# Mixture of experts, Mamba block, mixture of experts on one core: scan states in SBUF, masking on ScalarE, decays two steps ahead, residual adds on TensorE

## The reference

```python
# xn = rmsnorm(layernorm(x)) on 256 features; D_INNER 512, D_STATE 16, D_CONV 4, DT_RANK 64
x_in, z = split(xn @ in_proj_w.T)
x_conv  = silu(causal_conv4(x_in) + conv_b)
dt_low, B_ssm, C_ssm = split(x_conv @ x_proj_w.T)         # 64, 16, 16
dt = softplus(dt_low @ dt_proj_w.T + dt_proj_b);  A = -exp(A_log)
h  = h * exp(dt_t * A) + (dt_t * u_t) * B_t               # for every t; 512 x 16 states
y  = sum_s h[:, s] * C_t[s]  + x_conv * D
x  = x + (y * silu(z)) @ out_proj_w.T                     # x here is the layernormed input
h  = rmsnorm(x);  x = x + relu(h @ c_fc_w.T)**2 @ c_proj_w.T
```

## Time and profile before

| | us |
|---|---|
| median of 3 runs | 2183.04 |
| lowest and highest | 2175.22, 2190.57 |
| the profiled execution, its time | 2182.28 |
| its span, first to last instruction | 2180.4 |
| first scan to last product's end | 591.8 to 1607 |
| VectorE busy over the span | 1709.5 (78%) |
| TensorE busy | 1725.6 (79%) |
| GpSimd busy | 1242.9 (57%) |
| ScalarE busy | 977.6 (45%) |

### The profile page before, as it was taken

One profiled execution on the slowest core, in us unless ns is written; L12 is line 12 of the kernel. 1 busy time (PEld: TensorE's weight loads), 2 busy tenths in 40 slices (PEclk: granted clock), 3 DMA queues, 4 the chain that ended last, 5 costly groups with the idle time before them and its releaser, 6 DMA issues. The chain is left out here.

```text
span 2180.4 us, 35658 instructions
## 1 busy us (share of the span) xinstructions
PE 1725.6 (79%) x10728; PEld 1411.5 (65%) x10729; DVE 1709.5 (78%) x2990; ACT 977.6 (45%) x1507; POOL 1242.9 (57%) x751
## 2 busy tenths in 40 slices
PE   5279999993886878879787787877577379999996
PEld 5279999993344546545464554545456269999996
DVE  4857666665498999989999999989955757766665
ACT  2333333331465566566666656665431323333331
POOL 1257455555476767767676676767631246545555
PEclk8589999997877898989999898988686579999998
DMA  6244343343343434434344443443412334333342
GB/s 193 79 120 105 69 86 82 82 70 90 121 137 126 140 127 141 136 122 143 127 136 127 137 136 127 136 128 136 142 36 97 97 102 106 81 74 87 82 78 26
DMA packets 161018, 237.96 MB, mean 109 GB/s; under 512 B 29370, under 2 KB 85296, under 8 KB 160304
## 3 DMA queue, kind: packets, MB, share of 16 engines
q1 hardware_dynamic: 130096, 198.84, 28.7%
q0 software_dynamic: 30720, 36.53, 10.1%
HBM read 202.57 MB, written 38.34 MB: 110 GB/s over the span
## 5 line engine op out<-in xcount | busy, mean ns | idle before, releaser
L1291 POOL TENSOR_TENSOR m_dB<-m_DTU,m_BC 128x1024 f32<-128x1024 f32 x256 | 604.0, 2362 | 308.0 <-DVE PS L1397 307.5
L1397 DVE TENSOR_TENSOR_SCAN PS<-PS,m_ST,m_dB 128x512 f32<-128x512 f32 x512 | 628.3, 1271 | 58.7 <-POOL m_dB L1291 27.1
L1110 ACT ACTIVATE PS<-m_DT,m_A 128x512 f32<-128x512 f32 x512 | 351.1, 690 | 361.3 <-DVE PS L1397 360.1
L1101 PEld LDWEIGHTS PS<-keep_ident,m_G 128*128 128x128 f32 x2048 | 254.9, 153 | 207.8 <-DVE m_G L1406 168.2
L1101 PE MATMUL PS<-keep_ident,m_G 128*128 128x128 f32 x2048 | 313.5, 297 | 90.2 <-DVE m_G L1406 89.7
L1406 DVE TENSOR_TENSOR m_G<-PS,m_BC 128x512 f32<-128x512 f32 x512 | 340.8, 673 | 10.3 <-PE PS L1101 10.2
L603 PE MATMUL PS<-e_xh,e_wh 128*128 128x256 f32 x1008 | 295.0, 293 | 0.5 <-DVEq L491 0.2
L603 PE MATMUL PS<-e_xl,e_wh 128*128 128x256 f32 x1008 | 289.0, 287 | 0.0
L603 PE MATMUL PS<-e_xh,e_wl 128*128 128x256 f32 x1008 | 288.8, 287 | 0.0
L660 ACT ACTIVATE e_hh<-e_u 128x512 fp32r<-128x512 f32 x252 | 157.9, 633 | 281.1 <-DVE e_u L716 280.9
L621 PE MATMUL PS<-e_wh,e_hh 128*128 128x256 f32 x1008 | 281.4, 279 | 0.0
(11 more groups left out here) (200 smaller groups left out, 2908.1 us busy)
## 6 DMA issues: line engine op xcount, KB each, us to landing
m_BC<-bc_rows SPq DMA_DIRECT2D x512, 256.0 KB, 3.3
layer_raw<-w SPq DMA_DIRECT2D x64, 512.0 KB, 3.9
xrows<-r_xn SPq DMA_DIRECT2D x16, 512.0 KB, 4.2
keep_X<-x SPq DMA_DIRECT2D x4, 1024.0 KB, 9.6
sums<-keep_X SPq DMA_DIRECT2D x4, 1024.0 KB, 11.1
out<-keep_X SPq DMA_DIRECT2D x4, 1024.0 KB, 11.0
keep_X<-sums SPq DMA_DIRECT2D x3, 1024.0 KB, 13.4
e_xin<-xrows,e_gix POOLq DMA_INDIRECT x160, 3.3
```

Of the source, the lines that this page charges most:

```text
L1101: last = M(PS[:, B_Y + j, ts], G[:, s % 2, j, ts], C["ident"][:, :], is_transpose=True, start=False, stop=(s == DS - 1 and a == CTT - 1))
L1110: return nc.scalar.activation(out, in_, func, **kw)
L1291: G_.tensor_tensor(dB[:, s % 2, :, :], DTU[:, es, :], BC[:, s % NBC, 0:1, :].to_broadcast([P, 2, CT]), ALU.mult).then_inc(dB_ok, 1)
L1397: V.tensor_tensor_scan(PS[:, B_H + j, :], PS[:, B_DA + j, :], dB[:, s % 2, j, :], ST[:, s, e:e + 1], ALU.mult, ALU.add).then_inc(scanned, 1)
```

## The change

- The scans write a new SBUF tensor `HS` (two buffers of two blocks), and the products read it there; PSUM banks 4 and 5 become free and hold a second pair of decays, which ScalarE computes two steps ahead.
- The masked copy of the last state becomes a ScalarE activation with a 0/1 scale (`keep`), behind that step's decays; a scan waits for the `keep` of two steps back.
- `G` has four buffers for two.
- `out` and `pj`: TensorE first multiplies the residual rows by the identity into the bank and then adds the projection onto it; ScalarE copies the bank out. VectorE has no instruction in the tables any more.
- `v`: the 1/256 goes into ScalarE's squares, eps is added by GpSimd.
- To make room, `T3` and `HID` share one tensor (`TH`), and `hT` is `xrT`.

```diff
-        mask = sb("mask", [P, MCH + 1], U32)
-        fmask = sb("fmask", [P, MCH])
+        fmask = sb("fmask", [P, MCH + 1])
...
-        G = sb("G", [P, 2, 2, CT])
+        NG, NH = 4, 2
+        G = sb("G", [P, NG, 2, CT])
+        HS = sb("HS", [P, NH, 2, CT])
...
-        B_DA, B_H, B_Y = 2, 4, 6
+        B_DA, B_Y, AHEAD = 2, 6, 2
...
         BACK = {
...
-            ("out", 0): (4, _, 5, _), ("out", 1): (6, _, 7, _), ("sq", 0): (_, 9, _, _), ("v", 0): (_, _, 10, 12),
+            ("out", 0): (4, 5, _, _), ("out", 1): (6, 7, _, _), ("sq", 0): (_, 9, _, _), ("v", 0): (_, _, _, 11),
...
-            ("fc", 3): (27, 28, _, _), ("q", 1): (_, 28, _, _), ("pj", 0): (29, _, 30, _), ("pj", 1): (30, _, 31, _),
+            ("fc", 3): (27, 28, _, _), ("q", 1): (_, 28, _, _), ("pj", 0): (29, 30, _, _), ("pj", 1): (30, 31, _, _),
...
                     if kind == "out":
                         wait_read(pe, k, ("g", 2), ("g", 3), into=p)
+                        pe.wait_ge(xn_ok, k + 1)
+                        rows = XP[:, 2 * n:2 * n + 2, :]
                     else:
                         pe.wait_ge(q_ok, k * 2 + 2)
+                        pe.wait_ge(xa_ok, k * 2 + (n + 1 + XA0))
+                        rows = X[:, bass.ds(k * CTT + 2 * n, 2), :]
+                    M(bank(p, k), C["ident"][:, :], rows.rearrange("p t d -> p (t d)"), start=True, stop=False)
...
-                        last = F(XR[:, t, :], XP[:, t, :], ACT.Square, accum_out=ssq[:, t:t + 1])
+                        last = F(XR[:, t, :], XP[:, t, :], ACT.Square, scale=1.0 / math.isqrt(D), accum_out=ssq[:, t:t + 1])
...
-                    if not (is_first(k) and n == 0):
-                        act.wait_ge(scanned, k * (2 * STEPS) + (2 * (n - 1) + j + 1))
-                    F(PS[:, B_DA + j, :], DT[:, e, :], ACT.Exp, scale=A[:, e, s:s + 1]).then_inc(dA_ok, 1)
+                    if not (is_first(k) and n < AHEAD):
+                        act.wait_ge(scanned, k * (2 * STEPS) + (2 * (n - AHEAD) + j + 1))
+                    F(PS[:, B_DA + 2 * (n % AHEAD) + j, :], DT[:, e, :], ACT.Exp, scale=A[:, e, s:s + 1]).then_inc(dA_ok, 1)
+
+            def keep(k, p, s):
+
+                n = p * DS + s
+                F(ST[:, s, 2 * p:2 * p + 2], HS[:, n % NH, :, CT - 1], ACT.Copy, scale=fmask[:, bass.ds(k + 1, 1)]).then_inc(kept, 1)
...
                 if kind == "v":
+                    gp.wait_ge(sq_ok, k + 1)
+                    G_.tensor_tensor(ssq[:, :], ssq[:, :], eps[:, :], ALU.add).then_inc(v_ok, 1)
...
-                if kind == "out":
-
-                    dve.wait_ge(xn_ok, k + 1)
-                    wait_written(dve, p, k)
-                    xp = XP[:, 2 * n:2 * n + 2, :]
-                    V.tensor_tensor(xp, xp, bank(p, k).rearrange("p (t d) -> p t d", t=2), ALU.add).then_inc(read(p, k), 1)
-                elif kind == "v":
-                    dve.wait_ge(sq_ok, k + 1)
-                    V.tensor_scalar(ssq[:, :], ssq[:, :], 1.0 / D, RMS_EPS, ALU.mult, ALU.add).then_inc(v_ok, 1)
...
-                            if not (is_first(k) and n == 0):
-                                dve.wait_ge(g_ok, k * (2 * STEPS) + (2 * n + j - 1))
-                                dve.wait_ge(kept, k * STEPS + n)
+                            if not (is_first(k) and n < NH):
+                                dve.wait_ge(g_ok, k * (2 * STEPS) + (2 * (n - NH) + j + 1))
+                                dve.wait_ge(kept, k * STEPS + (n - NH + 1))
...
-                            V.tensor_tensor_scan(PS[:, B_H + j, :], PS[:, B_DA + j, :], dB[:, s % 2, j, :], ST[:, s, e:e + 1],
+                            V.tensor_tensor_scan(HS[:, n % NH, j, :], PS[:, B_DA + 2 * (n % AHEAD) + j, :], dB[:, s % 2, j, :], ST[:, s, e:e + 1],
...
-                            V.tensor_tensor(G[:, s % 2, j, :], PS[:, B_H + j, :], BC[:, s % NBC, 1, :], ALU.mult).then_inc(g_ok, 1)
+                            V.tensor_tensor(G[:, n % NG, j, :], HS[:, n % NH, j, :], BC[:, s % NBC, 1, :], ALU.mult).then_inc(g_ok, 1)
...
-                        dve.wait_ge(scanned, k * (2 * STEPS) + (2 * n + 2))
-                        V.tensor_tensor(ST[:, s, 2 * p:2 * p + 2].bitcast(U32), PS[:, B_H:B_H + 2, CT - 1].bitcast(U32),
-                                        mask[:, bass.ds(k + 1, 1)].to_broadcast([P, 2]), ALU.bitwise_and).then_inc(kept, 1)
```

More of the change, by code:

```diff
@@ L1 @@
+import math
 import concourse.bass as bass
@@ L789, in mamba, with hid @@
         mhalf = sb("mhalf", [P, 2, 2 * CTT])
+        eps = sb("eps", [P, CTT])
         XI = sb("XI", [P, EK, DC - 1 + CT])
         U = sb("U", [P, 2, EK, CT])
-        T3 = sb("T3", [P, EK, CT])
-        HID = sb("HID", [P, EK, CT])
+        TH = sb("TH", [P, 6, CT])
+        T3 = TH[:, 0:EK, :]
+        def hid(e, n=1):
+            at = e + 4 if e < 2 else e
+            return TH[:, at:at + n, :]
         xrT = sb("xrT", [P, DK, CT])
-        hT = sb("hT", [P, DK, CT])
+        hT = xrT
         XR = sb("XR", [P, CTT, D])
@@ L1061, in back @@
                 elif kind in ("out", "pj"):
-                    at, src = (W_OUT, T3) if kind == "out" else (W_PJ, HID)
+                    at, src = (W_OUT, lambda e: T3[:, e:e + 1, :]) if kind == "out" else (W_PJ, hid)
                     if kind == "out":
                         wait_read(pe, k, ("g", 2), ("g", 3), into=p)
+                        pe.wait_ge(xn_ok, k + 1)
+                        rows = XP[:, 2 * n:2 * n + 2, :]
                     else:
                         pe.wait_ge(q_ok, k * 2 + 2)
+                        pe.wait_ge(xa_ok, k * 2 + (n + 1 + XA0))
+                        rows = X[:, bass.ds(k * CTT + 2 * n, 2), :]
+                    M(bank(p, k), C["ident"][:, :], rows.rearrange("p t d -> p (t d)"), start=True, stop=False)
                     for t in (2 * n, 2 * n + 1):
                         for e in range(EK):
-                            last = M(bank(p, k)[:, (t % 2) * D:(t % 2 + 1) * D], src[:, e, t * P:(t + 1) * P],
-                                     weights(at, D, e, 0, D), start=(e == 0), stop=(e == EK - 1))
+                            last = M(bank(p, k)[:, (t % 2) * D:(t % 2 + 1) * D], src(e)[:, 0, t * P:(t + 1) * P],
+                                     weights(at, D, e, 0, D), start=False, stop=(t % 2 == 1 and e == EK - 1))
                 elif kind == "hT":
@@ L1190, in back @@
                 kind, n = p
-                if kind == "sq":
+                if kind == "out":
+                    wait_written(act, p, k)
+                    F(XP[:, 2 * n:2 * n + 2, :].rearrange("p t d -> p (t d)"), bank(p, k), ACT.Copy).then_inc(read(p, k), 1)
+                elif kind == "pj":
+                    wait_written(act, p, k)
+                    act.sem_inc(joined, 1)
+                    x = X[:, bass.ds(k * CTT + 2 * n, 2), :]
+                    F(x.rearrange("p t d -> p (t d)"), bank(p, k), ACT.Copy).then_inc(read(p, k), 1)
+                elif kind == "sq":
                     wait_read(act, k, ("out", 0), ("out", 1))
                     for t in range(CTT):
-                        last = F(XR[:, t, :], XP[:, t, :], ACT.Square, accum_out=ssq[:, t:t + 1])
+                        last = F(XR[:, t, :], XP[:, t, :], ACT.Square, scale=1.0 / math.isqrt(D), accum_out=ssq[:, t:t + 1])
                     last.then_inc(sq_ok, 1)
@@ L1301, in _ @@
             V.memset(mhalf[:, :, :], -0.5)
-            V.memset(fmask[:, :], 1.0)
-            link(V.memset(mask[:, :].bitcast(mybir.dt.int32), -1))
+            V.memset(eps[:, :], RMS_EPS)
+            link(V.memset(fmask[:, :], 1.0))
             V.memset(ST[:, :, :], 0.0)
@@ L1306, in _ @@
             for k in range(0, MCH, MCH // BATCH):
-                V.memset(fmask[:, k:k + 1], 0.0)
-                link(V.memset(mask[:, k:k + 1].bitcast(mybir.dt.int32), 0))
+                link(V.memset(fmask[:, k:k + 1], 0.0))
             def tile(k, t, n=1):
@@ L1369, in back @@
                 kind, n = p
-                if kind == "out":
-                    dve.wait_ge(xn_ok, k + 1)
-                    wait_written(dve, p, k)
-                    xp = XP[:, 2 * n:2 * n + 2, :]
-                    V.tensor_tensor(xp, xp, bank(p, k).rearrange("p (t d) -> p t d", t=2), ALU.add).then_inc(read(p, k), 1)
-                elif kind == "v":
-                    dve.wait_ge(sq_ok, k + 1)
-                    V.tensor_scalar(ssq[:, :], ssq[:, :], 1.0 / D, RMS_EPS, ALU.mult, ALU.add).then_inc(v_ok, 1)
[L1379 to L1383, removed]
+                return
             def turn(k, par, has_front, has_back):
```

23 lines of the change are left out of this document (13 added, 10 removed).

## The result

| | us |
|---|---|
| changed kernel, median of 4 runs | 2635.49 (2629.59 to 2645.05) |
| kernel before, median of 4 runs beside it | 2184.43 (2175.22 to 2190.57) |
| ratio, 95% interval | 1.208 [1.205, 1.212] |
| span of the profiled execution | 2629.0 (before 2180.4) |
| selective scan, first scan to last scan's end | 1460.0 (before 1014.4) |

The change made the kernel a fifth slower. The forecast was 2215 us, and 2635 lies outside its range of 2100 to 2240. The second rival, with a chance of 0.12, had 2673 us and the mechanism that the trace shows.

What follows compares the result with a forecast made beforehand. The prediction took VectorE to bound the selective scan, busy 970.7 of 1015.2 us. It summed 2182.3 - 17 - 16 - 8.5 - 35 + 108 + 2 = 2215.8, say 2215 us, range 2100 to 2240.

Steps and rivals of the forecast that it cites:

- The second rival: Selective scan: dB gets in between a step's two products, every step 5.86 us, 2673 us in all; chance 0.12.
- a VectorE pair stays together: Selective scan: GpSimd never goes between a step's two products; part of the main forecast of 2215 us, chance 0.54.
- dB waits for it, and runs under the next two scans: Plain scan steps: GpSimd's dB starts after the product pair and fits, 2.31 us in 2.37.
- The exclusion itself: Selective scan: VectorE's SBUF products and GpSimd's products block each other, whoever comes first finishes; 2215 us with it, 2107 without.
- The 108 us for GpSimd's other operations: Selective scan: product pairs wait for GpSimd work around dB: 67 us adds and DTU, 21 pow and X adds, 20 L1365.
- the 20 beside L1365: Selective scan, 15 times: dB starts beside L1365 and the product pair waits 1.36 us, 20 us together.
- The mask, the adds and the eps step: Selective scan: work taken off VectorE, saving 17 us for the mask, 16 for residual adds, 8.5 for eps.
- The 2 us for the drain: Behind the last step: four identity products of 0.59 us each on TensorE lie on the path, +2 us.
- The waits taken off: Selective scan: longer decay lead and four product buffers remove 35 of 38.6 us of VectorE's waits for ScalarE and TensorE.
- No exclusion: Rival, selective scan: SBUF products never wait for GpSimd, the 108 us fall away, 2107 us; chance 0.20.
- only GpSimd is held up: Rival, selective scan: VectorE never waits for a running product and just slows GpSimd; 2190 us, no change; chance 0.12.
- A slower scan: Selective scan: the scan into SBUF takes longer than its 1.19 us; what is left of the chances, 0.02.

Runs made afterwards that it cites:

- Experiment 3: Changed kernel with GpSimd's dB waiting for both products of two steps before instead of for the scans; 2232.91 us, 1.023 times the kernel before.
- experiment 1: Kernel before with only the scans writing SBUF and mask and products reading it there; 2656.54 us, 1.217 times the kernel before.
- experiment 5: Changed kernel with dB computed for only the first 256 of each chunk's 512 tokens, the rest left out; 2370.50 us.
- experiment 2: Changed kernel with scans back in PSUM, mask back on VectorE and one step of lead; 2164.26 us, ratio 0.993 to the kernel before.
- the memset: Changed kernel with a GpSimd memset of 64 columns and its semaphore between the wait for the scans and dB; 2618.36 us.
- 192 columns: Changed kernel with a GpSimd memset of 192 columns for 64 between the wait for the scans and dB; 2285.90 us, 1.048 times before.
- experiment 4: Changed kernel with a step's two products made by one VectorE instruction of 128x1024; 2556.65 us, 1.171 times the kernel before.

## Why the prediction was wrong

**The step that failed** is the premise "that a VectorE pair stays together", and with it "dB waits for it, and runs under the next two scans". A pair is two instructions, and GpSimd can go between them. dB starts early in the first product, goes at its end in 239 steps of 256, and the second waits 2.83 - 0.68 = 2.15 us: 532 us over the stage with the few others. Experiment 3, with pairs kept by force, gave 2233 us where the forecast said 2215; experiment 1 has the loss with no other part of the change.

**How I came to it.** I read it from one meeting in the routing stage: a pair of L302, GpSimd's L341 starting inside the first, and the second not put off. That meeting is real, and it repeats: four times in each of the eleven traces, with L341 0.130 to 0.149 us ahead of the second L302, which is never put off. But the same trace of the kernel before has 26 meetings that went the other way, and I overlooked them. In two neighbouring L298, 24 times with no semaphore's wait between them, L341 starts inside the first one and the second one waits for it, 707 to 761 ns for 242. Where L341 comes in a row of eight, the two engines simply alternate:

```profile
79.08 5.47 POOL L341 TENSOR_TENSOR r_hot<-r_count,r_high 128x320 f32<-128x320 f32 x8 [41.22 <-DVEq L288]
79.11 5.49 DVE L298 TENSOR_SCALAR r_inlow<-r_count_b,r_low 128x128 bf16<-128x128 bf16 x8 [0.46 <-DVE r_high L287]
```

Eight L298 take 5.49 us where one alone takes 0.24. I had this in the earlier trace rows as "up to 761 ns for 242", and took it for who comes first and not for what happens between two VectorE instructions. The four favourable meetings against the 26 should have moved the rival far above 0.12.

**What was right.** The exclusion itself, and its price, the rest of GpSimd's instruction (experiment 5). The 108 us for GpSimd's other operations: 88 comparable, 86 measured in experiment 3, and for the 20 beside L1365 the changed kernel has 15 first products at 1.93 to 2.01 us for 0.66, which is 19. The scan in SBUF costs what it did. The mask, the adds and the eps step left VectorE as costed: 1329 instructions became 1039. The sum of the stage closes with them: 1014.4 - 17 - 16 - 8.5 - 44.5 of waits + 532 = 1460.4 for the measured 1460.0. The 2 us for the drain can't be told: from the last scan's end to the block's last write it is 42.0 us before and 45.6 in the changed kernel, but experiment 1, with the old adds, has 45.8.

**What was off in size.** The rival's own 2673 us is 38 too high: I let the second product wait for all of dB, 2.31 us, and it waits 2.15. dB begins its work a little before the second product is due, and the product ends only 0.55 us behind dB, less than its own 0.68. A step is 5.70 us instead of 5.86; times 256, this is 41 us. The waits taken off are not 35 us but all 44.5 in the changed kernel, where the long steps hide everything, the loop's turns too; but where steps are short (experiment 3) a new one appears: the masked copy stands in ScalarE's queue behind the silu block, and VectorE waits 17.0 us for it at steps 22 and 24, in the row

```profile
DVE m_HS L1417 <- ACT m_ST L1126: 17.0, 14, 1.7
```

I had costed that copy at 0, since "the result is due two steps later".

**What of the rivals.** "No exclusion" and "only GpSimd is held up" are both out: VectorE's products wait (2851 ns), and so does dB (2710 for 2344). "A slower scan" is out as well.

## What to carry to other kernels

Before an operand moves from PSUM to SBUF on VectorE, look at what GpSimd reads at that moment: here a VectorE instruction with two SBUF inputs waited out what was left of a GpSimd instruction, however small it was itself, and the wait shows as busy time. Where both must meet, fix the order by a semaphore, as experiment 3 did with one wait, or by who reads from PSUM, as experiment 2. And a sequence of instructions is not a unit: ask of each boundary who may be waiting there, and before one favourable meeting becomes a rule, count all meetings of the kind in the trace, those of other instructions too.

## What the runs showed of the hardware

- VectorE with two SBUF inputs and GpSimd reading SBUF exclude each other for a whole instruction, both ways: 2.83 us for 0.68, 2.30 for 0.14, and dB 2.91 for 2.36 (3.43 behind one product of 1.23). With one operand in PSUM neither is slowed (0.67 and 2.36 us at the same meeting).
- The order is decided anew for each instruction, also between two VectorE instructions that overlap in the records (239 of 256 pairs split). With the memset ahead of it, dB had to start some 0.11 to 0.12 us ahead of the second one to be in time. This is no general threshold: two dB of the first chunk split a pair at 0.055 us (changed kernel) and 0.027 us (192 columns), and L341 got between two L298 at 0.007 to 0.076 us.
- Where both wait for the same event, 0.05 us one way or 0.01 us the other decide who goes first (experiment 4).
- Reading SBUF instead of PSUM made the product hardly faster (minimum 654 ns for 660), and writing SBUF took 10 ns off the scan's mean (1261 for 1271).
- Why L341 lost to the second L302 at 0.130 to 0.149 us, where dB got in at 0.111 and L341 itself in front of an L298 at 0.007, is open; the instructions differ in operation, shape and operands, and I did not vary these.
